# A four-stage attention and feed-forward kernel on one core: GpSimd's weight rounding and late layer-norm scales split into single operations

## The chip, the core and the metric

The kernel runs on one core of one Trainium2 chip. The metric is the device time of one execution in microseconds. Before the change the median of three runs is 936.67 us (935.26 to 936.72).

## The reference, cut to what matters

The input `x` has 128 sequences of 64 tokens with 128 features. Four residual stages follow each other, each on a layer norm of `x`:

```python
x = x + tanh(g_xattn[0]) * L0_xattn(layernorm(x), ctx, ctx)   # 16 heads of 8
x = x + tanh(g_ffn[0])   * L0_ffn(layernorm(x))               # 4 experts, 128 -> 256 -> 128, gated per token
x = x + tanh(g_xattn[1]) * L1_xattn(layernorm(x), ctx, ctx, mask)
x = x + tanh(g_ffn[1])   * L1_ffn(layernorm(x))               # ternary weights, conv over 3 tokens, silu

def weight_quant(w):                                          # used for w1 and w2 of L1_ffn
    scale = 1.0 / clip(mean(abs(w)), 1e-05)
    return clip(round(w * scale), -1, 1) / scale
```

In the second stage every token mixes the outputs of its chosen experts, each with its bias, by softmax weights. In the last stage activations are quantised per token to 8 bits and the weights `w1` (128 x 512) and `w2` (512 x 128) to -1, 0 or 1.

## The kernel before, in words

All of `x` stays in SBUF as `x_all`: 64 tiles (T) of 128 tokens by 128 features, in 16 groups (NG) of 4 (G). The stages are first attention (about 0 to 270 us), experts (to about 497 us), second attention (to about 765 us) and the feed-forward stage ("ffn", to the end). Each engine has a program of its own, written out in full; engines meet only in semaphores (`wait` at a count, `then_inc` when an instruction is done). The order of an engine's work is therefore the order in which the code emits it: `run_tiles` calls a step function for t from `first` to T + `lag` and calls `before[t]` ahead of step t; `lead_in` emits some steps of a later stage inside an earlier one. A step asks `has(k)` whether tile or group t + k exists, so work of several tiles is interleaved.

**Experts.** One step u handles group u. TensorE (`experts`, L1557 and on) emits eight hidden products (`hidden`, L1535 to L1537, three matmuls of 512 columns each), the gate matmuls (L1541), the transposes of the next group (L1357) and, in between, `y_tile(u - 1, j)` for the four tiles of the group before (L1522, 16 matmuls each). `y_tile(u - 1, 0)` waits until all hidden units of group u - 1 have been through relu: five of the eight on ScalarE (L744), three on VectorE (L1113), the last of them number 7. `y_tile` of tile t also waits until the tile two before it has been combined. VectorE (`experts`, L1153 and on) computes the gate (L1047 to L1104, the last writes the mixing weights `gwt`), adds the four expert outputs into `x_all` (`combine`, L1124, four operations a tile; the first waits for `eb_added`) and collects layer-norm statistics (L1143, L1147). ScalarE multiplies the four expert biases by the weights (`bias_products`, L736). GpSimd (`experts`, L497 and on) adds those products and puts them into `x_all` (`add_biases`, L503, L506, L509; two tiles of group u - 1, then two of group u) and computes four small layer-norm scale operations for group u + 3 (L519), for which it waits on VectorE's L1147.

**Rounding the last stage's weights.** `f_w1` and `f_w2` (128 x 512 each) are rounded on GpSimd by `ternary` (L560): three operations each (multiply by the scale and add the rounding constant, L564; subtract it and cap at 1, L566; floor at -1, L568). The scales `f_s` come from VectorE's `ffn_scales` (L1244: L1246, L1248, L1250, L1251). `ternary(f_w1)` stands ahead of GpSimd's step 13 (NG - 3), behind four lead-in steps of the second attention; `ternary(f_w2)` stands ahead of step 14. The rounded weights are first read in the second attention, by `tap_weights` (L579) on GpSimd and `copy_w2` on ScalarE. `ffn_scales` and four lead-in steps (`bn_stats` L1004, `bn_aggr` L1013) stand ahead of VectorE's step 12 (NG - 4); four more lead-in steps stand ahead of step 13.

**Feed-forward.** Step t on TensorE emits nine convolution matmuls of tile t (`conv_tap`, L1664 to L1666), the transpose of the quantised tile t + 2 (`transpose_xq`, through L1357, input `xdq`) and four output matmuls of tile t - 4 (L1689). The transposed tile is copied by ScalarE (L874, L875 `tap_hi`). GpSimd's `ffn(t)` (L601) emits in this order: `tap_lo` (L608, waits for ScalarE's `tap_hi`), `q2` (L616), `xdq` (L623), at t = 2, 4 and 8 a whole `ln_group`, and `xn` of tile t + 4 (L632). `ln_group(pool, g)` (L262; its operations are recorded on L265) computes the layer-norm scales of a group in four operations: `ln_ve` and `ln_nm`, then a power of -1/2 `ln_rs`, then `ln_nr`. Groups 0 to 12 are done in the second attention, groups 13, 14 and 15 at t = 2, 4 and 8 of the ffn stage; those are tiles 52 to 63, first used at t = 48.

Of the kernel before, what the change touches and what calls it, by code (L numbers as in the profile page):

```python
# [10 lines left out]
ALU = mybir.AluOpType  # L11
# [15 lines left out]
G = 4  # L27
NG = T // G
# [9 lines left out]
ROUND = 1.5 * 2.0 ** 23  # L38


C_ID, C_ONE, C_J, C_H, C_TIE, C_THR, C_POW, C_RND, C_EPS, C_NEG, C_ID2, C_NRND = \
# [4 lines left out]
def build(nc, a, out):  # L46

    with ExitStack() as ctx:
# [39 lines left out]
        f_w1 = sb("f_w1", [P, F])  # L88
        f_w2 = sb("f_w2", [P, FC, D])
# [5 lines left out]
        f_s = sb("f_s", [P, 8])  # L95
# [3 lines left out]
        ln_mv = sb("ln_mv", [P, 4, G, 2])  # L99
        ln_ve = sb("ln_ve", [P, G])  # L100
# [102 lines left out]
        def wait(eng, name, value):  # L203

            if isinstance(value, int) and value <= 0:
                return
            eng.wait_ge(s[name], value)
# [7 lines left out]
        def lead_in(step, first, last, T=T, mod=2):  # L215

            for t in range(first, last + 1):
                step(t, t % mod, lambda k: 0 <= t + k < T)
# [25 lines left out]
        LN_STEPS = 4  # L244
# [16 lines left out]

        def ln_group(pool, g):  # L262

            def stat(out, a, b, op):
                pool.tensor_tensor(out, a, b, op).then_inc(s["ln_ready"], 1)  # L265

            def all_tiles(c):
                return const[:, c:c + 1].to_broadcast([P, G])

            tiles = slice(G * g, G * (g + 1))  # L270
            wait(pool, "ln_mv", G * (g + 1))
            wait(pool, "ln_ready", LN_STEPS * g)
            stat(ln_ve[:], ln_mv[:, g % 4, :, 1], all_tiles(C_EPS), ALU.add)
            stat(ln_nm[:], ln_mv[:, g % 4, :, 0], all_tiles(C_NEG), ALU.mult)
            wait(pool, "ln_ready", LN_STEPS * g + 2)
            stat(ln_rs[:, tiles], ln_ve[:], all_tiles(C_POW), ALU.pow)
            wait(pool, "ln_ready", LN_STEPS * g + 3)
            stat(ln_nr[:, tiles], ln_nm[:], ln_rs[:, tiles], ALU.mult)

# [119 lines left out]
        def _(pool):  # L399
# [97 lines left out]
            def experts(u, par, has):  # L497
# [13 lines left out]
                if has(-1):  # L511
                    add_biases(-1, 2)
                    add_biases(-1, 3)
                if has(3):

# [43 lines left out]

            def ternary(w, i):  # L560

                k = TERN_DVE + 3 * i
                pool.wait_ge(s["tern"], k)
                pool.tensor_scalar(w, w, f_s[:, 4 + i:5 + i], ROUND, ALU.mult, ALU.add).then_inc(s["tern"], 1)  # L564
                pool.wait_ge(s["tern"], k + 1)
                pool.tensor_scalar(w, w, -ROUND, 1.0, ALU.add, ALU.min).then_inc(s["tern"], 1)  # L566
                pool.wait_ge(s["tern"], k + 2)
                pool.tensor_scalar(w, w, -1.0, 0.0, ALU.max, ALU.add).then_inc(s["tern"], 1)  # L568

# [11 lines left out]
            def tap_lower():  # L581
# [12 lines left out]
            run_tiles(pool, experts, 3, 1, T=NG, first=-1, before={  # L594
                NG - 3: lambda: (lead_in(attention1, -8, -5, mod=8), ternary(f_w1[:], 0)),
                NG - 2: lambda: ternary(f_w2[:].rearrange("p c d -> p (c d)"), 1)})
            pool.wait_ge(s["setup_v"], 2)
# [3 lines left out]
            def ffn(t, par, has):  # L601
# [16 lines left out]
                if has(2):  # L618
# [5 lines left out]
                        .then_inc(s["xq_ready"], 1)  # L624
                if t in (2, 4, 8):
                    ln_group(pool, {2: NG - 3, 4: NG - 2, 8: NG - 1}[t])
                if t >= 2 and has(4):
# [310 lines left out]
        def _(dve):  # L938
# [314 lines left out]
            def first_bias():  # L1253
# [15 lines left out]
            run_tiles(dve, experts, 3, 0, T=NG, first=1, before={  # L1269
                NG - 4: lambda: (ffn_scales(), lead_in(attention1, -12, -9, mod=8)),  # L1270
                NG - 3: lambda: lead_in(attention1, -8, -5, mod=8),
# [541 lines left out]
```

## Time and profile before

| | before |
|---|---|
| median of 3 runs | 936.67 us |
| lowest, highest | 935.26, 936.72 us |
| profiled execution, its own time | 936.35 us |
| its span | 934.5 us |
| what lies around the span | 1.85 us |
| TensorE busy | 906.0 us (97% of the span) |
| VectorE busy | 811.1 us (87%) |
| ScalarE busy | 742.8 us (79%) |
| GpSimd busy | 652.9 us (70%) |

In the views PE is TensorE, PEld its weight loads, DVE is VectorE, ACT ScalarE, POOL GpSimd and SP the engine that issues the transfers. A line of a timeline gives start (us from the start of the span), duration (us), engine, line of the kernel, operation, output<-inputs with partitions x elements, how many instructions are merged into it, and in brackets for how long the engine sat idle before it and who ended that. A line of the waits gives who waited for whom: us in total, how many times, the longest. A matmul's duration is from issue to its modelled end, so consecutive matmuls overlap; where the next instruction starts says more than where one ends.

### The profile page before, as it was taken

How to read it: one execution, taken by the hardware profiler on the slowest of the kernel's cores; microseconds unless marked ns; L12 is line 12 of the kernel's file. 1: busy time of each engine (PE TensorE's matmuls, PEld its weight loads, DVE VectorE, ACT ScalarE, POOL GpSimd, SP SyncE). 2: the span in 40 equal slices, each digit the busy share in tenths (PEclk: the TensorE clock that was granted, in tenths of full speed). 3: DMA queues.
4: the chain of work that ended last, by engine and by line, in shares of the span. 5: the costliest groups of instructions: out<-in, count | busy, mean ns of one | idle time of the engine just before them, and what ended most of it. 6: DMA issues, size and time to landing. Idle time of an engine off the chain costs nothing. (4 is left out here: it accounts for less than half of the span.)

```text
span 934.5 us, 32489 instructions
## 1 busy us (share of the span) xinstructions
PE 906.0 (97%) x11654; PEld 736.1 (79%) x11654; DVE 811.1 (87%) x2348; ACT 742.8 (79%) x1617; POOL 652.9 (70%) x1184
## 2 busy tenths in 40 slices
PE   6999999999999999999899999999999999999996
PEld 3888788788889999998786777777777777777774
DVE  6898888899979998899778988898988868888886
ACT  5888888888887777776676788788878877888885
POOL 5787878776635566565989878778786638777773
PEclk9999999999999999999999999999999999999999
DMA  3501010100000000000000000000000003333333
GB/s 117 189 26 48 26 47 26 47 14 26 13 2 2 1 1 2 1 1 1 2 13 14 14 26 14 26 14 14 26 14 14 4 7 66 82 78 80 78 78 82
DMA packets 54270, 31.15 MB, mean 33 GB/s; under 512 B 38368, under 2 KB 46816, under 8 KB 54112
## 3 DMA queue, kind: packets, MB, share of 16 engines
q1 hardware_dynamic: 54112, 29.08, 11.7%
q8 instruction: 95, 1.56, 0.7%
q14 instruction: 63, 0.52, 0.2%
HBM read 16.48 MB, written 4.19 MB: 22 GB/s over the span
## 5 line engine op out<-in xcount | busy, mean ns | idle before, releaser
L1011 DVE TENSOR_REDUCE smax<-score 128x16 f32<-128x1024 f32 x128 | 156.6, 1224 | 44.7 <-PE score L1441 23.9
L1382 PEld LDWEIGHTS bank<-vb,prob_t 128*64 128x64 f32 x4096 | 130.2, 138 | 49.4 <-issue 40.9
L1023 DVE TENSOR_TENSOR prob<-score,smax 128x512 f32<-128x512 f32 x256 | 163.4, 680 | 0.4
L657 ACT ACTIVATE prob_t<-bank 128x512 f32<-128x512 f32 x256 | 139.1, 595 | 20.2 <-PE bank L1357 6.5
L652 ACT ACTIVATE prob<-prob 128x512 f32<-128x512 f32 x256 | 147.5, 632 | 5.4 <-DVE prob L1023 5.4
L1382 PE MATMUL bank<-vb,prob_t 128*64 128x18 f32 x4096 | 142.5, 212 | 0.1
L1357 PE MATMUL bank<-const,prob 128*128 128x128 f32 x1024 | 133.8, 274 | 0.7 <-DVE x_all L1124 0.7
L1357 PEld LDWEIGHTS bank<-const,prob 128*128 128x128 f32 x1024 | 116.4, 141 | 1.8 <-DVE x_all L1124 1.1
L736 ACT ACTIVATE eb_t<-eb,gwt 128x128 f32<-128x128 f32 x256 | 81.5, 390 | 40.0 <-POOL eb_acc L503 26.3
L663 ACT ACTIVATE o_t<-bank,b_col 128x128 f32<-128x128 f32 x128 | 48.8, 381 | 65.9 <-PE bank L1357 65.7
L435 POOL TENSOR_SCALAR kj<-k_sb,const 128x512 f32<-128x512 f32 x124 | 85.2, 694 | 20.7 <-issue 20.7
L1441 PE MATMUL score<-kj,q_sb 32*64 32x256 f32 x2048 | 88.3, 400 | 2.8 <-DVE prob L1023 2.4
L1664 PE MATMUL score<-f_wk_hi,tap_hi 128*128 128x512 f32 x192 | 81.0, 422 | 0.2 <-DVE prob L1023 0.2
L1666 PE MATMUL score<-f_wk_hi,tap_lo 128*128 128x512 f32 x192 | 75.8, 395 | 0.0
L1665 PE MATMUL score<-f_wk_lo,tap_hi 128*128 128x512 f32 x192 | 75.5, 393 | 0.0
L1522 PE MATMUL bank<-ew,hid_b 128*128 128x128 f32 x512 | 62.5, 276 | 2.5 <-DVE hid_b L1113 2.5
L1522 PEld LDWEIGHTS bank<-ew,hid_b 128*128 128x128 f32 x512 | 60.6, 192 | 4.3 <-issue 2.8
L1522 PE MATMUL bank<-ew,hid_a 128*128 128x128 f32 x512 | 62.8, 276 | 0.4 <-DVE x_all L1124 0.4
L1394 PE MATMUL bank<-w_t,o_t 128*128 128x128 f32 x256 | 62.3, 325 | 0.9 <-DVE x_all L979 0.9
L1522 PEld LDWEIGHTS bank<-ew,hid_a 128*128 128x128 f32 x512 | 60.8, 192 | 2.9 <-DVE x_all L1124 1.1
L608 POOL TENSOR_TENSOR tap_lo<-x_t,tap_hi 128x128 fp32r<-128x128 f32 x64 | 26.3, 411 | 47.6 <-ACT tap_hi L875 47.6
L882 ACT ACTIVATE q2b<-hid_b,const 128x512 bf16<-128x512 f32 x64 | 46.2, 723 | 15.3 <-POOL hid_b L616 11.7
(171 smaller groups left out, 2335.3 us busy)
## 6 DMA issues: line engine op xcount, KB each, us to landing
ctx_t<-in_ctx SPq DMA_DIRECT2D x32, 256.0 KB, 2.7
x_all<-in_x SPq DMA_DIRECT2D x16, 256.0 KB, 3.4
out_x<-x_all SPq DMA_DIRECT2D x64, 64.0 KB, 1.8
ew<-in_ew SPq DMA_DIRECT2D x2, 512.0 KB, 6.0
q2t<-q2b SPq DMA_TRANSPOSE x64, 2.5
f_cw<-in_f_cw SPq DMA_DIRECT2D x1, 768.0 KB, 7.6
w_t<-in_w_attn SPq DMA_DIRECT2D x2, 256.0 KB, 4.2
f_w<-in_f_w SPq DMA_DIRECT2D x2, 256.0 KB, 7.0
```

Source lines behind the costliest of these rows:

```text
L435: pool.tensor_scalar(kj[:, gp, h, :], k_sb[:], const[:, C_J + h:C_J + h + 1], 0.0, ALU.mult, ALU.add).then_inc(s["kj_ready"], 1)
L652: act.activation(v, v, ACT.Exp, scale=SCALE).then_inc(s["exp_done"], 1)
L657: act.activation(prob_t[:, 4 * half:4 * half + 4, :].rearrange("p i q -> p (i q)"), bank[(PT, PT2)[half]], ACT.Copy).then_inc(s["p_copied" ...
L736: act.activation(eb_t[:, j % 2, e, :], eb2[:, e * P:(e + 1) * P], ACT.Copy, scale=gwt[:, gp, j, e:e + 1]).then_inc(s["eb_mult"], 1)
L1011: dve.tensor_reduce(smax[:].rearrange("p (r h) -> p r h", r=RH), sc, AX.X, ALU.max).then_inc(s["smax_done"], 1)
L1023: dve.tensor_tensor(prob[:, par, half * 512:(half + 1) * 512].rearrange("p (r h k) -> p r h k", r=2, k=S), sc[:, g], m.unsqueeze(3).to_bro ...
L1357: return pe.transpose(dst, src, ident)
L1382: last = pe.matmul(bank[OV][q, i * 2 * VW:(i + 1) * 2 * VW], prob_t[:, i, q], vb[:, k // G, v0 + b * NPAIR + i, :, :].rearrange("p h v -> ...
L1441: last = pe.matmul(bank[r][q, 0:SW], q_sb[c, gpar, g], kj[c, gpar, :, g], start=(L == 0), stop=True, skip_group_check=True)
L1522: last = pe.matmul(bank[6 + j % 2][:, e * P:(e + 1) * P], hid[gpar][:, 2 * e + c, j * P:(j + 1) * P], ew2[:, 2 * e + c, :], start=(c == 0) ...
L1664: pe.matmul(bank[par], hi, f_wk_hi[:, tap, :], start=(tap == 0), stop=False)
L1666: last = pe.matmul(bank[par], lo, f_wk_hi[:, tap, :], start=False, stop=(tap == TAPS - 1))
```

## The change

`ternary` emits one of its six operations at a call, and GpSimd's experts step u calls it for u = 4 to 9, between `add_biases(u - 1, 3)` and the layer-norm scales of group u + 3; the two calls ahead of steps 13 and 14 are gone. `ffn_scales` on VectorE moves from ahead of step 12 to ahead of step 2. In the ffn stage the twelve operations of the three late layer-norm groups are emitted one a step, t = 2 to 13, at the place where the whole group stood. The operations themselves are the same.

```diff
-        def ln_group(pool, g):
+        def ln_part(pool, g, part):
...
             tiles = slice(G * g, G * (g + 1))
-            wait(pool, "ln_mv", G * (g + 1))
-            wait(pool, "ln_ready", LN_STEPS * g)
-            stat(ln_ve[:], ln_mv[:, g % 4, :, 1], all_tiles(C_EPS), ALU.add)
-            stat(ln_nm[:], ln_mv[:, g % 4, :, 0], all_tiles(C_NEG), ALU.mult)
-            wait(pool, "ln_ready", LN_STEPS * g + 2)
-            stat(ln_rs[:, tiles], ln_ve[:], all_tiles(C_POW), ALU.pow)
-            wait(pool, "ln_ready", LN_STEPS * g + 3)
-            stat(ln_nr[:, tiles], ln_nm[:], ln_rs[:, tiles], ALU.mult)
+            wait(pool, "ln_ready", LN_STEPS * g + (0, 0, 2, 3)[part])
+            if part == 0:
+                wait(pool, "ln_mv", G * (g + 1))
+                stat(ln_ve[:], ln_mv[:, g % 4, :, 1], all_tiles(C_EPS), ALU.add)
+            elif part == 1:
+                stat(ln_nm[:], ln_mv[:, g % 4, :, 0], all_tiles(C_NEG), ALU.mult)
+            elif part == 2:
+                stat(ln_rs[:, tiles], ln_ve[:], all_tiles(C_POW), ALU.pow)
+            else:
+                stat(ln_nr[:, tiles], ln_nm[:], ln_rs[:, tiles], ALU.mult)
+
+        def ln_group(pool, g):
+            for part in range(LN_STEPS):
+                ln_part(pool, g, part)
...
                 if has(-1):
                     add_biases(-1, 2)
                     add_biases(-1, 3)
+                if 4 <= u < 10:
+                    ternary(u - 4)
                 if has(3):
...
-            def ternary(w, i):
+            def ternary(k):
...
+                i, part = k // 3, k % 3
+                w = (f_w1[:], f_w2[:].rearrange("p c d -> p (c d)"))[i]
+                pool.wait_ge(s["tern"], TERN_DVE + k)
...
             run_tiles(pool, experts, 3, 1, T=NG, first=-1, before={
-                NG - 3: lambda: (lead_in(attention1, -8, -5, mod=8), ternary(f_w1[:], 0)),
-                NG - 2: lambda: ternary(f_w2[:].rearrange("p c d -> p (c d)"), 1)})
+                NG - 3: lambda: lead_in(attention1, -8, -5, mod=8)})
...
-                if t in (2, 4, 8):
-                    ln_group(pool, {2: NG - 3, 4: NG - 2, 8: NG - 1}[t])
+                if 2 <= t < 14:
+                    ln_part(pool, NG - 3 + (t - 2) // LN_STEPS, (t - 2) % LN_STEPS)
...
             run_tiles(dve, experts, 3, 0, T=NG, first=1, before={
-                NG - 4: lambda: (ffn_scales(), lead_in(attention1, -12, -9, mod=8)),
+                2: ffn_scales, NG - 4: lambda: lead_in(attention1, -12, -9, mod=8),
```

## Rows read from the trace of the kernel before

**Rows 1.** The profile page: busy time by engine, and TensorE's granted clock in 40 slices.
```profile
PE 906.0 (97%) x11654; PEld 736.1 (79%) x11654; DVE 811.1 (87%) x2348; ACT 742.8 (79%) x1617; POOL 652.9 (70%) x1184
...
PEclk9999999999999999999999999999999999999999
```

**Rows 2.** The waits of TensorE over the whole span, two of its rows.
```profile
PE bank L1357 <- POOL xdq L623: 2.7, 3, 1.1
PE bank L1522 <- DVE hid_b L1113: 2.5, 1, 2.5
```

**Rows 3.** The timeline of TensorE, 443 to 458 us.
```profile
443.40 0.63 PE L1357 MATMUL bank<-const,m_xn 128*128 128x128 f32 x4 [0.47 <-DVE gl L1047]
...
450.78 2.05 PE L1522 MATMUL bank<-ew,hid_a 128*128 128x128 f32 x16 [0.41 <-DVE x_all L1124]
...
454.06 1.00 PE L1541 MATMUL bank<-gate_w,mxt 128*128 128x68 f32 x8
457.53 2.02 PE L1522 MATMUL bank<-ew,hid_b 128*128 128x128 f32 x16 [2.47 <-DVE hid_b L1113]
```

**Rows 4.** The timeline of VectorE, 424 to 457 us.
```profile
424.83 0.16 DVE L1246 RECIPROCAL f_s<-f_s 128x2 f32<-128x2 f32 x1
...
425.27 0.29 DVE L1004 BATCH_NORM_STATS2 a_st<-x_all 128x6 f32<-128x128 f32 x1
...
449.55 0.53 DVE L1090 TENSOR_TENSOR g_ew<-g_sel,ge 128x16 f32<-128x16 f32 x1
...
450.85 0.23 DVE L1104 SCALAR_TENSOR_TENSOR gwt<-g_ew,tg,g_rs 128x16 f32<-128x16 f32 x1
455.26 0.35 DVE L1124 SCALAR_TENSOR_TENSOR y_acc<-bank,gwt,x_all 128x128 f32<-128x128 f32 x1 [4.18 <-POOL x_all L509]
...
456.68 0.74 DVE L1113 TENSOR_SCALAR hid_b<-score,eb 128x512 f32<-128x512 f32 x1
```

**Rows 5.** The timeline of GpSimd, 448 to 455 us.
```profile
448.65 0.69 POOL L564 TENSOR_SCALAR f_w<-f_w,f_s 128x512 f32<-128x512 f32 x1
449.43 1.95 POOL L566 TENSOR_SCALAR f_w<-f_w 128x512 f32<-128x512 f32 x1
451.47 1.94 POOL L568 TENSOR_SCALAR f_w<-f_w 128x512 f32<-128x512 f32 x1
453.37 0.73 POOL L503 TENSOR_TENSOR eb_acc<-eb_t 128x256 f32<-128x256 f32 x1
...
454.72 0.45 POOL L509 TENSOR_TENSOR x_all<-x_all,eb_sum 128x128 f32<-128x128 f32 x1
```

**Rows 6.** GpSimd's waits, 320 to 420 us, and the first of them on its timeline.
```profile
POOL m_ve L519 <- DVE m_mv L1147: 31.6, 7, 4.6
...
324.89 0.20 POOL L519 TENSOR_TENSOR m_ve<-m_mv,const 128x4 f32<-128x4 f32 x1 [4.11 <-DVE m_mv L1147]
```

**Rows 7.** VectorE's waits for TensorE, 296 to 424 us.
```profile
DVE y_acc L1124 <- PE bank L1522: 7.3, 15, 0.6
```

**Rows 8.** The timeline of GpSimd in the ffn stage, step t = 4 and a later step.
```profile
772.79 0.20 POOL L265 TENSOR_TENSOR ln_ve<-ln_mv,const 128x4 f32<-128x4 f32 x1
...
773.22 1.01 POOL L265 TENSOR_TENSOR ln_rs<-ln_ve,const 128x4 f32<-128x4 f32 x1
774.32 0.20 POOL L265 TENSOR_TENSOR ln_nr<-ln_nm,ln_rs 128x4 f32<-128x4 f32 x1
774.49 0.45 POOL L632 TENSOR_SCALAR xn<-x_all,ln_rs,ln_nr 128x128 f32<-128x128 f32 x1
...
782.43 0.41 POOL L608 TENSOR_TENSOR tap_lo<-x_t,tap_hi 128x128 fp32r<-128x128 f32 x1 [0.59 <-ACT tap_hi L875]
```

**Rows 9.** The timeline of TensorE in the ffn stage, the transposes of three steps.
```profile
772.89 0.33 PE L1357 MATMUL bank<-const,xdq 128*128 128x128 f32 x1
...
776.40 0.33 PE L1357 MATMUL bank<-const,xdq 128*128 128x128 f32 x1 [0.83 <-POOL xdq L623]
...
778.93 0.27 PE L1357 MATMUL bank<-const,xdq 128*128 128x128 f32 x1
```

More of the change, by code:

```diff
@@ L558, in _ @@
             attention1 = attention(1)
-            def ternary(w, i):
[L562 to L568, printed above, removed]
+            def ternary(k):
+                i, part = k // 3, k % 3
+                w = (f_w1[:], f_w2[:].rearrange("p c d -> p (c d)"))[i]
+                pool.wait_ge(s["tern"], TERN_DVE + k)
+                if part == 0:
+                    pool.tensor_scalar(w, w, f_s[:, 4 + i:5 + i], ROUND, ALU.mult, ALU.add).then_inc(s["tern"], 1)
+                elif part == 1:
+                    pool.tensor_scalar(w, w, -ROUND, 1.0, ALU.add, ALU.min).then_inc(s["tern"], 1)
+                else:
+                    pool.tensor_scalar(w, w, -1.0, 0.0, ALU.max, ALU.add).then_inc(s["tern"], 1)
             def tap_scales():
```

## The prediction

> **What bounds the kernel now.** I read the page first: TensorE is busy for 97% of the span, at a granted clock of nine tenths or more in every slice, so at its 2.4 GHz level [rows 1]. VectorE is second with 87%. GpSimd, whose program is what changes, is busy 70% of the time. So nothing on GpSimd counts by its length. It counts only where TensorE, directly or through another engine, stands still for it. The second view is therefore the waits of TensorE. Of its idle time two entries lead back to the work that is moved [rows 2]: one stall of 2.5 us for a relu of VectorE, and three of together 2.7 us for `xdq` of GpSimd. The third view, the timelines around these stalls, shows who was late.
>
> At 457.53 TensorE has been idle for 2.47 us; it wants `y_tile(13, 0)` and lacks relu 7 of group 13 [rows 3]. That relu ran at 456.68, behind a combine that VectorE had in front of it, and VectorE itself had sat idle 4.18 us for GpSimd's L509 [rows 4]. GpSimd had spent 448.65 to 453.37 on the three roundings of `f_w1` before it began those biases [rows 5]. So the chain is ternary, bias add, combine, relu, matmul, and its head is 4.72 us long.
>
> In the ffn stage the transposes stand at 772.89, 776.40 and 778.93 [rows 9]: steps of 3.51 and 2.53 us. The long one follows a whole layer-norm group on GpSimd, 772.79 to 774.49 [rows 8].
>
> **Part 1: the roundings leave steps 13 and 14.** Removed ahead of step 13: 4.72 us of GpSimd [rows 5]. The bias add of the waited tile takes 453.37 to 454.72 + 0.45 = 455.17, so 1.80 us; started at 448.65 it ends at 450.45. What is late next? VectorE's weights `gwt` end at 450.85 + 0.23 = 451.08 [rows 4], so the combine starts there instead of at 455.26, 4.18 us earlier, and relu 7, which ends at 456.68 + 0.74 = 457.42, would end at about 453.24. On ScalarE the bias products (four in 1.2 to 1.3 us) and one relu of 0.67 us, both behind `gwt`, end near 453.0. TensorE comes to this point at about 457.53 - 2.47 = 455.06. The margin is 1.8 us, so the whole stall goes: 2.5 us. The second set of roundings, ahead of step 14, costs TensorE nothing listed now; I count nothing for it. Bounds of this part: 2.5 us is all there is, and if VectorE kept the stall it would be 0.
>
> **Part 2: `ffn_scales` goes from step 12 to step 2.** It occupies VectorE from 424.83 to 425.27, 0.44 us [rows 4]. After it VectorE is late through steps 12 and 13: TensorE waits for it 0.47 us at 443.40 and 0.41 us at 450.78 [rows 3]. Both have VectorE's two lead-ins as their main cause, and those stay. VectorE has no listed wait between 425 and 451, so it is 0.44 us earlier throughout, and TensorE gains that: 0.4 us, between 0 and 0.88. At step 2 the same 0.44 us is covered: VectorE waits for TensorE 15 times, 7.3 us, from there to step 12 [rows 7]. If that cover were gone it would cost at most 0.44 us, once. Its other wait, for the mean weights, was met long before.
>
> **Part 3: one rounding ahead of the scales of steps 4 to 9.** GpSimd gains four operations of 1.95 us and two of 0.69 us [rows 5]. They stand where it waits for VectorE's statistics: seven waits of 31.6 us in all, 4.5 us on average, the first 4.11 us [rows 6]. The longest rounding leaves at least 2.1 us. Behind it on GpSimd are the four scale operations and then two bias adds, and none moves while that idle time holds. If it did not hold, bias adds, combines and then `y_tile` would follow. Cost 0. The added waits on the semaphore `tern` are met a group earlier, except for the first, which needs `ffn_scales`, two steps earlier. No transfer is issued in anything that moves and nothing passes the SP queue.
>
> What the roundings may do to VectorE beside them is not free by itself. Under L566 (449.43 to 451.38, [rows 5]) VectorE's `g_ew`, with two inputs in SBUF, took 0.53 us [rows 4], while small operations of this size there take 0.2 us. So I bound it at 0 to 0.4 us of VectorE per rounding; VectorE's waits for TensorE are 7.3 us in about nine groups, 0.8 us a group [rows 7], and hold that. Taken: 0 for TensorE.
>
> The Trainium skill (SBUF — State Buffer, section "Who interferes with whom") says that a VectorE instruction with two SBUF inputs and a GpSimd instruction that reads SBUF contend for a shared pair, and that the one that issued second is blocked for the whole instruction. The trace does not agree for this rounding: `g_ew` was over at 450.08, 1.3 us before L566 was. By the rule `g_ew` alone would have lost 1.8 us there, and the sum would have to carry a loss in each of the four long roundings.
>
> **Part 4: one late layer-norm operation to a step.** Today the group takes GpSimd from 772.79 to 774.49, 1.70 us [rows 8], and makes TensorE's step 3.51 instead of 2.53 us, 0.98 us more [rows 9] (0.83 listed as idle, the rest in gaps too small to be listed). So 0.72 us is absorbed; 0.59 us of it is the idle time before `tap_lo` in an undisturbed step [rows 8]. Three groups cost about 2.9 us. After the change nine steps get an operation of 0.20 us, which takes 0.2 to 0.3 us of the queue: below 0.72, free. Three steps (t = 4, 8, 12) get the power, from 773.22 to 774.32, 1.10 us, less 0.72 = 0.38 us each, 1.1 us together. Gain 2.9 - 1.1 = 1.8 us. Bounds: 2.9 us if even the power is absorbed; 0 if a power alone costs what a group costs.
>
> **Sum.** 2.5 + 0.4 + 0 + 1.8 = 4.7 us, against the profiled execution's 936.35 us (934.5 us of span and 1.85 us around it), which is 0.3 us below the median of 936.67 us: 931.6 us. TensorE is the bound from 457 us to the end, and the transfers run far ahead, so what is gained stays gained.
>
> **The rivals.** A change within 0.2% (1.9 us, about what a measurement of this kernel can tell from none) is "same" here.
>
> A, the ffn part gives nothing, because the power alone holds the loop or because VectorE's late statistics (t = 2 to 6) take its place once GpSimd is no longer late. For it: an undisturbed step has only 0.59 us of idle time. Against it: three stalls become three shorter ones. 936.35 - 2.9 = 933.4 us. Chance 0.12.
>
> B, a wait takes the place of the one removed: VectorE or ScalarE, late from the lead-ins, holds `y_tile(13, 0)` anyway, and only about 1 of 2.5 us comes. Against it stands the margin of 1.8 us. 936.35 - 1.0 - 1.8 + 0.5 = 934.1 us, with no gain from part 2 and some of the new delay. Chance 0.07.
>
> C, better: the power is absorbed and the two small stalls at 443 and 451 us go entirely: 936.35 - 2.5 - 0.9 - 2.9 = 930.0 us. Chance 0.13.
>
> D, the change does nothing that reaches TensorE's end, since the gains are used up by waits of the second attention: 936.3 us. Against it: that stage waits only on VectorE and is entered in the same relation. Chance 0.04.
>
> E, slower. Each rounding of steps 4 to 9 blocks VectorE for its whole length, and VectorE, second busiest, passes it on. Price: 4 x 1.95 + 2 x 0.69 = 9.2 us, so 931.6 + 9.2 = 940.8 us. It decides from the point where more than half of it gets through; VectorE's spare 0.8 us a group and `g_ew`'s 0.53 us speak against it. This is what the skill's rule above would come to at its widest. Chance 0.02.
>
> The forecast has what is left, 0.62. The range takes in C less half a microsecond of scatter and reaches up over A and B: 929.4 to 934.3 us. Faster by over 0.2% means below 934.8 us: forecast, A, C and nearly all of B, 0.93; same 0.05; slower 0.02.
>
> **What would show it.** After the change: no entry for L1522 waiting on `hid_b` of 2 us or more, and VectorE no longer idle for L509 near 451 us; GpSimd's waits before L519 in steps 4 to 9 shorter by the rounding and still above 2 us; the waits at 443 and 451 us smaller by up to 0.4 us; three waits on `xdq` of about 0.2 to 0.4 us, at t = 4, 8 and 12, in place of three of 0.8 to 1.1. The prediction is wrong if TensorE shows new waits between 325 and 410 us, if the idle time at 457 us returns under another name, or if more than three steps of the ffn stage are longer than 2.6 us.

## The result, and the profile after

| | before | after |
|---|---|---|
| median, measured together (4 runs each) | 936.69 us | 928.94 us (928.12 to 929.59) |
| ratio | | 0.9919 [0.9905, 0.9934] |
| profiled execution, its own time | 936.35 us | 928.12 us |
| its span | 934.5 us | 926.3 us |
| VectorE busy | 811.1 us | 810.8 us |
| ScalarE busy | 742.8 us | 742.2 us |

The changed kernel is faster by 7.6 us [6.2, 8.9], where 5.1 us below the median (4.7 us below the profiled execution) was forecast; 928.94 lies just below the range (929.4 to 934.3). The prediction had the sign and the mechanisms, and not the size.

From the profile page of the kernel after, the busy times of all engines and TensorE's granted clock:

```profile
PE 903.7 (98%) x11654; PEld 734.8 (79%) x11654; DVE 810.8 (88%) x2348; ACT 742.2 (80%) x1617; POOL 653.1 (71%) x1184
...
PEclk9999999999999999999999999999999999999999
```

Set beside [rows 1], no engine has more or less to do: the counts of instructions are the same, and GpSimd's 653.1 us was 652.9. TensorE's busy time is 2.3 us less for the same 11654 matmuls; the execution before ran some of those in its start at a lower clock, as shown further down. What changed is when TensorE stands still. Its waits after (who waited for whom: us, times, longest), in the places of the two entries of [rows 2]:

```profile
PE bank L1366 <- POOL a_xn L438: 1.2, 1, 1.2
...
PE bank L1366 <- DVE x_all L1133: 0.7, 1, 0.7
PE bank L1531 <- DVE x_all L1133: 0.3, 1, 0.3
```

There is no entry for `hid_b` and none for `xdq` any more. The wait for `a_xn` is not a new one in their place: it stands at 13.5 us, in the start, and the unchanged kernel before shows it too in experiment 1 (1.2 us). TensorE's timeline after, around the place where it stood still for 2.47 us [rows 3]:

```profile
447.55 2.05 PE L1531 MATMUL bank<-ew,hid_a 128*128 128x128 f32 x16 [0.26 <-DVE x_all L1133]
...
450.83 1.00 PE L1550 MATMUL bank<-gate_w,mxt 128*128 128x68 f32 x8
451.67 2.00 PE L1531 MATMUL bank<-ew,hid_b 128*128 128x128 f32 x16
```

The 16 matmuls of `y_tile(13, 0)` follow the gate matmuls at once. On VectorE, in place of [rows 4]:

```profile
447.62 0.63 DVE L1113 SCALAR_TENSOR_TENSOR gwt<-g_ew,tg,g_rs 128x16 f32<-128x16 f32 x1
448.17 0.34 DVE L1133 SCALAR_TENSOR_TENSOR y_acc<-bank,gwt,x_all 128x128 f32<-128x128 f32 x1
...
449.59 0.74 DVE L1122 TENSOR_SCALAR hid_b<-score,eb 128x512 f32<-128x512 f32 x1
```

The combine starts as soon as `gwt` is written, with no idle time, and relu 7 ends at 450.33, 1.3 us before TensorE comes to it (a margin of 1.8 us was forecast). GpSimd at the place that a rounding moved to, and the waits there of GpSimd (317 to 418 us) and of VectorE for TensorE (290 to 418 us), in place of [rows 6, 7]:

```profile
331.27 0.46 POOL L515 TENSOR_TENSOR x_all<-x_all,eb_sum 128x128 f32<-128x128 f32 x1
331.70 1.95 POOL L576 TENSOR_SCALAR f_w<-f_w 128x512 f32<-128x512 f32 x1
336.18 0.20 POOL L527 TENSOR_TENSOR m_ve<-m_mv,const 128x4 f32<-128x4 f32 x1 [2.52 <-DVE m_mv L1156]
```
```profile
POOL m_ve L527 <- DVE m_mv L1156: 22.6, 7, 4.6
```
```profile
DVE y_acc L1133 <- PE bank L1531: 6.7, 15, 0.6
```

The rounding of 1.95 us leaves a wait of 2.52 us. The seven waits fell from 31.6 to 22.6 us, 9.0 us for six roundings that last 9.2 us together. VectorE's waits for TensorE stayed (7.3 and 6.7 us). So the six roundings lie entirely in time that was idle. VectorE's neighbour of that rounding, the mixing weights `gwt` with two inputs in SBUF, began and ended inside it:

```profile
333.17 0.22 DVE L1113 SCALAR_TENSOR_TENSOR gwt<-g_ew,tg,g_rs 128x16 f32<-128x16 f32 x1
```

In the ffn stage, GpSimd and TensorE at t = 4, in place of [rows 8, 9]:

```profile
765.47 0.38 POOL L632 TENSOR_SCALAR xdq<-q,sc_i 128x128 f32<-128x128 f32 x1
765.81 1.02 POOL L265 TENSOR_TENSOR ln_rs<-ln_ve,const 128x4 f32<-128x4 f32 x1
766.82 0.45 POOL L641 TENSOR_SCALAR xn<-x_all,ln_rs,ln_nr 128x128 f32<-128x128 f32 x1
```
```profile
765.90 0.33 PE L1366 MATMUL bank<-const,xdq 128*128 128x128 f32 x1
768.74 0.33 PE L1366 MATMUL bank<-const,xdq 128*128 128x128 f32 x1
771.27 0.27 PE L1366 MATMUL bank<-const,xdq 128*128 128x128 f32 x1
```

The step behind the power takes 2.84 us, the next one 2.53. No gap is large enough to be listed as idle.

**A ledger.** To find where 8.2 us went between the two profiled executions I cut both spans at the same five instructions of TensorE: A, from the start to the second group's gate matmuls (early in the experts); B, to the last group's gate matmuls; C, to the first transpose of `xdq`; D, over the next thirteen of these transposes, so thirteen steps (all three late groups of the kernel before are in it, and two of the three powers of the kernel after); E, the rest. Of B, the last distance is shown by itself, between the last two gate matmuls; it holds the stall. All numbers are differences of start times (the kernel before: 454.06 and 470.74 are the last two gate matmuls, so 16.68; after: 450.83 and 464.83, so 14.00). The same cuts serve for the kernels of the experiments.

```
us                                A       B (its last distance)  C       D      E      span
before                            270.43  200.31 (16.68)         279.59  42.23  141.94  934.5
after                             267.86  196.97 (14.00)         279.58  39.76  142.13  926.3
before, once more                 268.13  201.90 (18.30)         279.56  42.19  141.92  933.7
after, once more                  268.93  197.00 (14.03)         279.54  39.78  142.05  927.3
after, late groups whole          268.52  196.95 (13.99)         279.59  42.18  141.86  929.1
before + late LN in parts         269.03  201.92 (18.29)         279.58  39.76  142.21  932.5
before + ffn_scales moved         269.98  202.64 (19.52)         279.54  42.18  141.86  936.2
before, stall kept busy, 1st      269.25  200.29 (16.66)         279.58  42.18  141.90  933.2
before, stall kept busy, 2nd      267.97  200.39 (16.69)         279.63  42.24  142.07  932.3
after, second roundings late      269.03  196.94 (13.99)         279.56  39.75  142.02  927.3
after, roundings whole            269.81  197.00 (14.04)         279.58  39.76  142.05  928.2
after, power split                270.02  196.99 (14.00)         279.59  39.30  142.00  927.9
after, start kept busy            269.09  196.98 (13.99)         279.60  39.79  142.24  927.7
after, start busy, power split    270.06  196.99 (14.00)         279.59  39.34  141.92  927.9
```

Between the first two rows the change's own parts give 3.34 (B) + 2.47 (D) - 0.19 (E, where the third power makes a step of 2.75 us) = 5.6 us. The other 2.6 us are in A, in which nothing was changed. That is the question that the experiments start from: does the change reach back into A, or is A scatter, and what then is the kernel's real gain?

### The profile page after: what moved, and what is told of

Read it like the earlier page. It is cut to its first block and busy times, and to the rows that moved or that the text cites. A ratio compares the mean times of both kernels' runs of the same rounds, so it can differ in the third digit from the quotient of the medians.

```text
span 926.3 us, 32489 instructions
## 1 busy us (share of the span) xinstructions
PE 903.7 (98%) x11654; PEld 734.8 (79%) x11654; DVE 810.8 (88%) x2348; ACT 742.2 (80%) x1617; POOL 653.1 (71%) x1184
## 5 line engine op out<-in xcount | busy, mean ns | idle before, releaser
L1325 DVE TENSOR_TENSOR hid_b<-score,f_cb 128x512 f32<-128x512 f32 x64 | 44.3, 692 | 16.3 <-PE score L1675 16.2
```

## The experiments

Every run is compared with runs of the kernel before on the same chip. The median of the kernel before was 935.58 us (29 runs) beside experiments 1 to 4, 935.57 (15 runs) beside 5, 6, 8 and 9, and 936.03 (17 runs) beside 7 and 10 to 12. A kernel's profile is of one execution; its median is of all.

**1. The kernel before, unchanged.** The code is that of the kernel before, with no edit. It shows what scatter alone does to the ledger and to a comparison.

> The kernel before, unchanged, as a second copy. In the traces of before and after the second gate matmul of the experts (end of the first attention) starts at 270.43 and 267.86 us: 2.57 us apart, in a stretch where no instruction was changed. Theory 1 (chance): the start of the program falls out differently from execution to execution, whatever the kernel; then this copy is within 1 us of before in time, and its trace may show the second gate matmul anywhere from 267.8 to 270.5 us. Theory 2 (property of the program): a program has its own start; then this copy has about 270.4 us, in the trace and by its time (ratio 1.000).

Measured: 936.30 us (934.71 to 939.53, 12 runs), ratio 1.0006 [0.9994, 1.0018]. The kernel before scatters by almost 5 us, and its ledger moves in two places: A by 2.3 us, and the last distance of B by 1.6 us. So A is scatter. The second was not expected. TensorE's timeline of this run around the stall:

```profile
451.73 1.00 PE L1541 MATMUL bank<-gate_w,mxt 128*128 128x68 f32 x8
455.20 3.65 PE L1522 MATMUL bank<-ew,hid_b 128*128 128x128 f32 x16 [2.47 <-DVE hid_b L1113]
458.58 0.51 PE L1535 MATMUL score<-mx_hi,ew_hi 128*128 128x512 f32 x1
```

The stall is the same 2.47 us, but the 16 matmuls behind it take 3.65 us, where they took 2.02 us in [rows 3]. The reason is in the same stretch in windows (engine busy times, then TensorE's granted clock as a share, DMA share and GB/s), here of this run:

```profile
454.00:458.00 4.00, 2.80 (x13) 2.83 (x14) 3.82 (x12) 3.26 (x11) 3.40 (x7) 0.66 0.00 0
458.00:462.00 4.00, 4.00 (x29) 3.69 (x28) 3.75 (x14) 2.88 (x8) 3.76 (x5) 0.92 0.02 4
```

and of the execution that the prediction was read from:

```profile
454.00:458.00 4.00, 1.53 (x13) 1.37 (x13) 2.60 (x7) 3.70 (x10) 3.37 (x7) 1.00 0.00 0
458.00:462.00 4.00, 4.00 (x32) 3.69 (x32) 3.82 (x13) 3.26 (x11) 3.49 (x7) 1.00 0.00 0
```

A mean of 0.66 over 4 us is a stretch partly at the 1.2 GHz level. Behind the idle time of the stall the granted clock falls in this execution and did not in the other, and the fall costs another 1.6 us.

**2. The kernel after, with the late groups whole again.**

```diff
-                if 2 <= t < 14:
-                    ln_part(pool, NG - 3 + (t - 2) // LN_STEPS, (t - 2) % LN_STEPS)
+                if t in (2, 4, 8):
+                    ln_group(pool, {2: NG - 3, 4: NG - 2, 8: NG - 1}[t])
```

> The roundings and the weight scales moved as in the change, the late layer-norm groups whole as before. By the two traces the experts stage gained 3.3 us from the change (gap between second gate matmul and last gate matmul) and the ffn stage 2.3 us. Theory 1 (start by chance): 936.7 - 3.3 = 933.4 us. Theory 2 (the moved instructions change the start): 933.4 - 2.1 = 931.3 us, second gate matmul near 267.9 us. The forecast on record had 2.9 us for this part: 933.8 us.

Measured: 931.12 us (930.34 to 933.77, 6 runs), ratio 0.9947 [0.9931, 0.9963]. Its waits of TensorE, and two transposes:

```profile
PE bank L1366 <- POOL xdq L632: 2.7, 3, 1.1
```
```profile
767.62 0.33 PE L1366 MATMUL bank<-const,xdq 128*128 128x128 f32 x1
771.13 0.33 PE L1366 MATMUL bank<-const,xdq 128*128 128x128 f32 x1 [0.82 <-POOL xdq L632]
```

The three stalls of [rows 2] are back to the tenth, with the step of 3.51 us; D is 42.18 us. The roundings and the scales alone are worth 5.0 us [3.5, 6.5] by time, 2.9 us by the forecast. B, C and the last distance of B are the kernel after's within 0.02 us.

**3. The kernel before, with the late layer-norm operations one to a step.** The edit is the reverse of the one above, made in the kernel before, with `ln_group` divided into `ln_part` as in the change. The roundings stand three in a row ahead of steps 13 and 14 and the scales ahead of step 12, as before:

```diff
-                if t in (2, 4, 8):
-                    ln_group(pool, {2: NG - 3, 4: NG - 2, 8: NG - 1}[t])
+                if 2 <= t < 14:
+                    ln_part(pool, NG - 3 + (t - 2) // LN_STEPS, (t - 2) % LN_STEPS)
```

> Only the late layer-norm operations one to a step; roundings and scales where they were. Theory 1: 936.7 - 2.3 = 934.4 us. Theory 2, if the start follows from GpSimd's later code: 932.3 us; if it follows from VectorE's: 934.4 us. The forecast on record had 1.8 us for this part: 934.9 us. In its trace the steps with the power should be about 0.3 us longer than the others (2.84 and 2.75 against 2.53 us in the trace of after).

Measured: 934.31 us (933.26 to 937.38, 12 runs), ratio 0.9985 [0.9973, 0.9997], so a gain of 1.4 us [0.3, 2.5]. By the trace D is 39.76 us, the kernel after's to the hundredth, and E a little longer. TensorE's transposes:

```profile
772.02 0.33 PE L1365 MATMUL bank<-const,xdq 128*128 128x128 f32 x1
774.85 0.33 PE L1365 MATMUL bank<-const,xdq 128*128 128x128 f32 x1
```

The step with the power is 2.83 us long. D and E together give 2.47 - 0.27 = 2.2 us here. This part is independent of the others. Its stall at 456 us is there, and here too the clock fell behind it (the last distance of B is 18.29 us):

```profile
456.00:460.00 4.00, 3.87 (x18) 3.80 (x19) 3.86 (x13) 3.26 (x11) 3.54 (x7) 0.57 0.00 0
```

**4. The kernel before, with only `ffn_scales` moved to step 2.**

```diff
-                NG - 4: lambda: (ffn_scales(), lead_in(attention1, -12, -9, mod=8)),
+                2: ffn_scales, NG - 4: lambda: lead_in(attention1, -12, -9, mod=8),
```

> Only the four small scale operations on VectorE moved from ahead of step 12 to ahead of step 2. Forecast on record: 0.4 us, 936.3 us; from the gate matmuls of before and after (gaps 14.12 and 15.35 us before, 14.00 and 14.82 after) 0.6 us, 936.1 us, with the stall before relu 7 unchanged at 2.5 us, since GpSimd causes it. Theory 2, if the start follows from VectorE's code: 934.0 us.

Measured: 936.51 us (934.75 to 938.02, 12 runs), ratio 1.0003 [0.9992, 1.0014]: no difference that the times can tell. The trace can: B without its last distance is 202.64 - 19.52 = 183.12 us, and 183.63 us in the kernel before, so the move is worth 0.5 us. The wait of TensorE at 443 us (0.47 us) is gone; the next one is still there, 0.41 us at 449.81. The times can't show it, since this kernel has the clock's scatter as well. Its windows behind the stall are the worst of all:

```profile
456.00:460.00 4.00, 3.44 (x17) 3.48 (x17) 3.86 (x12) 3.25 (x11) 3.40 (x7) 0.50 0.00 0
458.00:462.00 4.00, 4.00 (x16) 3.62 (x16) 3.58 (x11) 2.18 (x8) 3.62 (x6) 0.50 0.00 0
```

At 0.50 for all of 456 to 462 us TensorE is at 1.2 GHz, with every matmul between; the last distance is 19.52 us, 2.8 us over the undisturbed 16.7. A stall of 2.46 us costs this execution 5.3 us.

**5. The kernel after, unchanged.** The code is that of the kernel after, with no edit.

> The changed kernel once more, beside more runs of before. In the runs so far the kernel before gives 933.97 to 938.53 us, and its copies show TensorE's granted clock at 0.5 to 0.6 (its 1.2 GHz level) for 2 to 6 us behind the stall that the roundings cause in step 14 (a gate matmul to gate matmul distance of 18.30 us in the second copy of before, 18.29 in the one with the layer norm alone, 19.52 in the one with the scales alone), and at 1.00 in the first profile (16.68). Theory C (clock): the roundings cost 2.6 us of stall plus 0 to 2.8 us of low clock, so the change is worth 2.7 + 0.6 + 1.7 on average in the experts and 2.3 in the ffn stage, 7.2 us in the mean of many runs, with clock 1.00 in its experts stage always. Theory S (the first 7.75 us came of a changed start): ratio as first measured, 0.9919, and a second gate matmul at 267.9 us again.

Measured: 929.18 us (928.91 to 929.9, 5 runs), ratio 0.9933 [0.9921, 0.9946], a gain of 6.3 us [5.1, 7.4]. A is 268.93 us this time; B, C, D and E are the same as before within 0.1 us. It scatters less than the kernel before: in no profile of a kernel without the stall is the last distance of B over 14.04 us.

**6. The kernel before, with TensorE kept busy where it stalls.** If the fall of the clock is a price of the stall over and above its length, it must go when the stall stays but TensorE isn't idle. Eleven products of the identity with itself, into a bank that nobody reads, stand behind the gate matmuls of the group with the stall (the view lists two matmuls for each, so 22):

```diff
+                if u == NG - 2:
+                    for _ in range(11):
+                        pe.matmul(bank[PT][:, 0:P], ident, ident, start=True, stop=True)
```

> The kernel before, with 11 matmuls of the identity (about 0.21 us each at the high clock, 2.3 us in all) emitted into an unused PSUM bank where TensorE stands idle 2.47 us in step 14. They add work that nothing needs and leave the stall itself as long as it was. Theory C: the clock stays at 1.00 there, gate matmul to gate matmul 16.7 us in the profile, and the time falls by the mean price of the low clock, 1 to 2 us: 934 us. Theory without the clock: no change or up to 0.3 us more, distance 16.7 or 18.3 us.

Measured: 935.12 us (933.4 to 936.42, 11 runs), ratio 0.9991 [0.998, 1.0002]. TensorE's timeline and the window:

```profile
453.72 2.67 PE L1568 MATMUL bank<-const 128*128 128x128 f32 x22
456.36 2.02 PE L1522 MATMUL bank<-ew,hid_b 128*128 128x128 f32 x16
```
```profile
454.00:458.00 4.00, 4.00 (x37) 3.87 (x36) 3.70 (x10) 3.82 (x12) 3.28 (x6) 1.00 0.00 0
```

`y_tile(13, 0)` starts no earlier: 3.48 us behind the gate matmuls (452.88 and 456.36), and 3.47 us in [rows 3]. Yet the clock is 1.00. The last distance is 16.66 us, as in the one execution of the kernel before in which the clock did not fall. By time the gain is 0.8 us, with zero in its interval, so I ran it again.

**7. The same kernel once more,** on another set of runs. There is no further edit.

> A second copy of the kernel before with 11 matmuls of the identity in the stall of step 14. The first gave 0.9991 [0.998, 1.0002] beside before, with a gate to gate distance of 16.66 us. Clock theory: again 16.7 us in the profile at clock 1.00, and 0.5 to 1.5 us faster than before (ratio 0.9984 to 0.9995). Without the clock: ratio 1.000 and a distance of 18 us in some profile.

Measured: 935.19 us (934.05 to 936.15, 12 runs), ratio 0.9987 [0.9977, 0.9997], a gain of 1.2 us [0.3, 2.2]. The last distance is 16.69 us, the clock 1.00 again. So both traces show the clock held; the mean price in time is about 1 us, and of the two intervals one begins at 0.3 us and the other holds zero. The long executions say the same: of the 61 runs of the kernel before beside the experiments 11 took over 937 us (up to 938.62), and of the 23 runs of these two copies none, the longest 936.42 us. The four profiles of kernels with the stall unfilled show 0, 1.6, 1.6 and 2.8 us, a mean of 1.5.

**8. The kernel after, with only the first set of roundings early.** It tells whether the second set, ahead of step 14, cost anything.

```diff
-                if 4 <= u < 10:
+                if 4 <= u < 7:
                     ternary(u - 4)
...
-                NG - 3: lambda: lead_in(attention1, -8, -5, mod=8)})
+                NG - 3: lambda: lead_in(attention1, -8, -5, mod=8),
+                NG - 2: lambda: [ternary(k) for k in range(3, 6)]})
```

> The change, but the roundings of f_w2 stay ahead of step 14 (f_w1's go to steps 4 to 6). The forecast on record priced the second set at nothing, since TensorE had no listed wait behind it. If that holds: same time as after, within 0.3 us, no stall near 460 us. If the second set only found TensorE late already because of the first, it now makes a stall of its own of up to 2.5 us in step 14 or 15, and 1 to 4 us with the clock: 930 to 933 us.

Measured: 928.98 us (928.1 to 929.13, 5 runs), ratio 0.9927 [0.9915, 0.994], not to be told from the kernel after. GpSimd rounds `f_w2` in one block again:

```profile
454.67 0.73 POOL L574 TENSOR_SCALAR f_w<-f_w,f_s 128x512 f32<-128x512 f32 x1
455.48 1.93 POOL L576 TENSOR_SCALAR f_w<-f_w 128x512 f32<-128x512 f32 x1
457.49 1.94 POOL L578 TENSOR_SCALAR f_w<-f_w 128x512 f32<-128x512 f32 x1
```

and TensorE's last distance is 13.99 us. These 4.8 us hold up nobody; the same block one step earlier cost 2.5 us of stall.

**9. The kernel after, with each set of roundings whole, in steps 4 and 5.** It tells whether the splitting matters or only the place.

```diff
-                if 4 <= u < 10:
-                    ternary(u - 4)
+                if 4 <= u < 6:
+                    for part in range(3):
+                        ternary(3 * (u - 4) + part)
```

> The change, but the three roundings of a weight in one step: f_w1 whole in step 4, f_w2 whole in step 5. They take 4.7 us of GpSimd where it is idle 4.1 to 4.5 us, so the scales behind them come at most 0.6 us late. If the place of the roundings is what counts: same as after within 0.3 us, no wait of TensorE between 320 and 420 us. If splitting them is what counts: bias adds, combines and y_tile of steps 4 and 5 come late and TensorE waits there, 0.5 to 2 us, possibly with its clock at the low level behind it.

Measured: 929.39 us (929.19 to 930.04, 5 runs), ratio 0.9935 [0.9923, 0.9948]. The waits of GpSimd from 317 to 418 us:

```profile
POOL m_ve L528 <- DVE m_mv L1157: 21.8, 5, 4.6
POOL eb_acc L509 <- POOL x_all L515: 0.4, 1, 0.4
```

In steps 4 and 5 the wait is used up whole, and the four scale operations start as soon as the last rounding ends. B is 197.00 us all the same. What counts is that the roundings leave step 13; that they come singly gains nothing measurable here.

**10. The kernel after, with the late power in two halves.** The power of four elements takes 1.02 us and still makes its step 0.3 us longer. Halved, each in a step of its own (fifteen steps, t = 2 to 16):

```diff
+        def ln_fifth(pool, i, k):
...
+                c = slice(2 * (k - 2), 2 * (k - 1))
+                wait(pool, "ln_ready", LN_STEPS * g + 2)
+                pool.tensor_tensor(ln_rs[:, G * g + c.start:G * g + c.stop], ln_ve[:, c],
+                                   const[:, C_POW:C_POW + 1].to_broadcast([P, 2]), ALU.pow)\
+                    .then_inc(s["ln_half" if k == 2 else "ln_ready"], 1)
...
-                if 2 <= t < 14:
-                    ln_part(pool, NG - 3 + (t - 2) // LN_STEPS, (t - 2) % LN_STEPS)
+                if 2 <= t < 17:
+                    ln_fifth(pool, (t - 2) // 5, (t - 2) % 5)
```

> The change, with the power of the three late groups cut in two operations of two tiles each, one to a step (15 steps, t = 2 to 16). In after, the steps with the power last 2.84, 2.76 and 2.75 us against 2.53 without. If a power of two elements takes about half of 1.02 us, it fits into the 0.6 to 0.7 us that a step leaves GpSimd and no step of the ffn stage is longer: the stretch of 13 transposes falls from 39.76 to 39.0 us, and the time by 0.7 us. If most of its time is a fixed cost, six steps are late in place of three: 39.8 to 40.5 us.

Measured: 928.98 us (927.75 to 929.67, 6 runs), ratio 0.9924 [0.9912, 0.9937]. GpSimd and TensorE:

```profile
768.03 0.70 POOL L297 TENSOR_TENSOR ln_rs<-ln_ve,const 128x2 f32<-128x2 f32 x1
```
```profile
768.11 0.33 PE L1381 MATMUL bank<-const,xdq 128*128 128x128 f32 x1
770.66 0.33 PE L1381 MATMUL bank<-const,xdq 128*128 128x128 f32 x1
```

Half the elements take 0.70 us, not half the time, and a step with them is 2.55 us. D falls from 39.76 to 39.30 us by the trace (the third power is in E); the time can't be told from the kernel after's.

**11. The kernel after, with the start kept busy.** The clock also falls in the first 24 us in some executions. Five identity products stand ahead of the first key projection's matmuls and five behind:

```diff
+            def fill(n):
+                for _ in range(n):
+                    pe.matmul(bank[PT][:, 0:P], ident, ident, start=True, stop=True)
...
+                            fill(5 if L == 0 else 0)
```

> The change, with five matmuls of the identity into an unused bank at each of two waits of TensorE in the first 20 us. In seven of ten profiles so far (of both kernels) the granted clock lies at 0.57 to 0.91 in one or both of the stretches 16:20 and 20:24 us, and the second gate matmul is then 254.4 to 254.8 us behind the first maximum of scores, against 254.0 us where the clock stayed at 1.00. If that is the start's clock: clock 1.00 there, distance 254.0, time 0.3 to 0.5 us less in the median. The other part of the start's scatter, the first maximum at 13.85 to 15.68 us, stays. If the added matmuls delay what TensorE waits for: up to 1 us more.

Measured: 929.98 us (929.54 to 932.25, 6 runs), ratio 0.9941 [0.9926, 0.9956], so nothing is gained. The clock was 1.00 from 16 to 24 us in the profile, as expected, but the distance from the first maximum of scores to the second gate matmul was 255.10 us, where 254.0 was expected, and A was 269.09 us. (In the ten profiles before, the clock was below 1.00 there in six, not in seven.) So it isn't shown that the low clock makes the long distance: either something else does, or the added matmuls cost what the clock gives back.

**12. Both of the last two edits together.**

> The change with the split power and the busy start together: 0.7 + 0.4 us below after, 928.1 us in the median, ratio to before 0.992.

Measured: 929.14 us (928.75 to 929.77, 6 runs), ratio 0.9928 [0.9916, 0.994], 1.0 us above what was expected. D is 39.34 us, A 270.06 us; the clock was again 1.00 from 16 to 24 us and the distance 254.61 us. No version beats the kernel after by more than the times can tell.

## Why the prediction was wrong

**What bounds the kernel, and the chain to the stall: right.** With the first set of roundings out of step 13 relu 7 is 1.3 us early, and the stall is gone from every kernel that lacks it there. That "the transfers run far ahead" was too much: in the last 9 us of both kernels TensorE waits 4.5 us in all for the transfers of `q2t`. It is the same in both and moves nothing in the sum.

**Part 1 (2.5 us): right but slightly small.** The last distance of B falls from 16.68 to 14.00 us and the rest of B, over and above what the scales give, by 0.15 us (183.12 to 182.97; it is the wait at 451 us, which goes from 0.41 to 0.26 us). Together 2.8 us. That the second set costs nothing was right (experiment 8).

**Part 2 (0.4 us): right, 0.5 measured** (experiment 4). It is the wait at 443 us alone, which is gone; the scales leave the one at 451 us as it was.

**Part 3 (0): right.** GpSimd lost 9.0 us of idle time and VectorE none that mattered, so rival E has nothing to stand on. The rule that VectorE and GpSimd block each other for whole instructions (the Trainium skill, SBUF — State Buffer, "Who interferes with whom") would have held back `gwt` in the kernel after: it reads two inputs from SBUF and started at 333.17 us, behind a rounding that lasted from 331.70 to 333.65. It took 0.22 us and was over at 333.39, before the rounding was. Nor does B grow (without its last distance 182.97 us after, 183.12 with only the scales moved), and VectorE is busy for 810.8 us where it was 811.1. The trace does not agree with the rule for these operations. The 0.53 us of `g_ew` that the prediction put down to a rounding are no proof of one either: beside the second set of roundings of the same execution, at 465.31 us, `g_ew` took 0.17 us.

**Part 4 (1.8 us): mechanism right, 2.3 measured** (2.47 from D, 0.19 back in E). The term that was too large is the power's: 1.10 less 0.72, so 0.38 us a step. The three steps took 2.84, 2.76 and 2.75 us against 2.45 to 2.53 beside them, so 0.2 to 0.4 us each and 0.8 together, where 1.1 stood in the sum. The 1.10 us were read inside a whole group, where the next operation waits for the power's result; in a step of its own the power holds GpSimd's queue from 765.81 to 766.82, 1.01 us. What was removed was 3.0 us, as forecast (2.9).

**The Sum: this is the step that failed.** It takes Part 1's stall at its length, 2.5 us, and the profiled execution as the typical one: "4.7 us, against the profiled execution's 936.35 us", "which is 0.3 us below the median". Two things are wrong in it, besides the 0.9 us by which the parts were small (3.34 + 2.47 - 0.19 = 5.6).

First, a term is missing, the clock. The prediction read "a granted clock of nine tenths or more in every slice" in the page [rows 1] and priced the stall at its length. In the execution shown that was its whole price. In three other profiles with the same stall TensorE ran at its lower level behind it, for 1.6 to 2.8 us more (experiments 1, 3 and 4), and with the stall filled it did not (6 and 7). The slices of the profile page are 23 us wide and hide 4 us at 0.66. The Trainium skill (TensorE: Matmul & The Clock Gate, "Why this matters for your kernels") lists idle gaps between bursts of matmuls as what lets the clock drop. The trace agrees in part: the clock fell, to a mean of 0.50 to 0.66 over 4 us, behind an idle time of 2.47 us, shorter than the gaps that the skill warns of, in three of four profiles, and in the fourth it did not. The mean price of the fall is 1.0 us by the times of experiments 6 and 7 and 1.5 by the profiles.

Second, the execution was taken as typical because its time was near the median. It was not: A took 270.43 us, where the six profiles of kernels with the stall have a mean of 269.1 us and those of the six without it, the start unfilled, 269.0. It started 1.3 us late and was spared the fall of the clock behind the stall, and the two cancelled. So what the medians saw go was not in the execution that the sum was made from.

Put right, with the parts as measured: 936.35 - 5.6 = 930.8 us; less the 1.3 us of late start, 929.4 us. Measured were 928.94 and 929.18. From the other side: a typical kernel before is 936.35 - 1.3 + 1.0 to 1.5 of clock = 936.1 to 936.6 us (measured 935.6 to 936.7). The gain is 5.6 + 1.0 to 1.5 = 6.6 to 7.1 us, and the two measurements of the unchanged kernels are 7.6 [6.2, 8.9] and 6.3 [5.1, 7.4].

**The rivals.** C, at 930.0 us, lay nearest, but for a reason that isn't there: it wanted the power absorbed and both small waits gone, and 0.8 us of the powers and 0.26 us of a wait remain. None of the rivals, nor the range, had a case in which the stall costs more than its length. The range's lower end was C less half a microsecond "of scatter", while the kernel before alone, unchanged, lay between 934.71 and 939.53 us in experiment 1.

**What stays open.** Why A scatters by 2.6 us isn't settled. Of the 2.57 us between the first two profiles 1.83 lie ahead of the first maximum of scores (VectorE starts it at 15.68 and 13.85 us) and 0.75 behind it. For those 0.75 us the clock is a candidate, which the slices of the profile page hid too:

```profile
16.00:20.00 4.00, 2.15 (x22) 1.06 (x21) 3.04 (x6) 1.80 (x3) 3.50 (x7) 0.84 0.28 70
20.00:24.00 4.00, 4.00 (x54) 2.42 (x54) 2.78 (x6) 3.11 (x6) 3.85 (x6) 0.73 0.00 0
```

This is the kernel before; after, both windows are at 1.00. In the other unfilled starts the distance is long where the clock was low as well, but experiments 11 and 12 held the clock and did not get the short distance. In the stretch ahead of the maximum two pieces are seen. In the execution before, VectorE's four operations on `kj` took 2.75 us, beside GpSimd's first products for `a_xn`, and in the one after 1.67 us:

```profile
9.76 2.75 DVE L956 TENSOR_SCALAR kj<-k_sb,const 128x512 f32<-128x512 f32 x4 [1.55 <-ACT k_sb L678]
```
```profile
8.98 1.67 DVE L965 TENSOR_SCALAR kj<-k_sb,const 128x512 f32<-128x512 f32 x4 [0.59 <-ACT k_sb L687]
```

and TensorE's first wait, for the constants from memory, was 4.4 and 4.0 us. The kernel before had 1.67 us there too in experiment 1, so neither belongs to the change. Over all fourteen profiles the four operations took 2.03 us or more in five, and in those the first maximum of scores starts at 15.18 us or later; in the other nine they took 1.67 or 1.68 us and it starts at 14.61 us or earlier. That two engines hinder each other in the first is likely from the overlap but wasn't tried. Nor is it known why the clock falls behind the stall in some executions and not in others.

## What to carry to other kernels

Cut two executions of the same kernel at the same instructions before making a sum against one of them: a time near the median doesn't say that each part is typical, and here a late start hid that a stall's further price was missing. Price a stall of TensorE by its length and by the matmuls behind it, in windows a few microseconds wide, since slices of the page are too coarse to show the clock. Work on an engine with long waits is free where it waits and dear one step ahead of a chain that ends at TensorE, and there the place counts more than how finely it is cut.

## What the runs showed of the hardware

A stall of 2.47 us of TensorE was enough for its granted clock to fall to the lower level for some microseconds, in three of four profiles, and eleven identity products in its place held it at 1.00 both times. In the start, the clock fell in several kernels around 16 to 20 us behind waits of 0.8 to 1.9 us (0.50 in experiment 10, 0.66 in experiment 5), and the matmuls there took twice as long.

GpSimd's `pow` costs 1.02 us for 128x4 and 0.70 us for 128x2, where its additions and products of 128x4 take 0.20 us. Its `tensor_scalar` on 128x512 takes 1.93 to 1.95 us with two immediate operands and 0.69 to 0.73 us where the first is a column of scalars, so the roundings' cost depends on their form. The slow ones also hold a minimum or a maximum, where the fast one multiplies and adds; which of the two differences counts wasn't tried. They cost nothing where they are.
